# Third layer of a four-layer recurrent model: the passage into its loop over channel tiles is rebuilt, work for the second sequence and the routing move into single steps of the loop, and three operations of a step change their order or their size

## The reference

```python
proj = x @ W_in.T + b_in                    # gate 2048 | h 2048, B 128, C 128 | dt 32
conv = sum(xp[:, i:i + S, :] * conv_w[:, i] for i in range(4))   # h, B and C
h, Bm, Cm = split(silu(conv))
dt = softplus(dt + dt_bias);  Adt = -exp(A_log) * dt
A_cum = cumsum(Adt)                         # within a chunk
Y_diag = einsum((C @ B.T) * exp(segsum(Adt)), h * dt)
states = recurrence over chunks of einsum(B * exp(A_cum[-1] - A_cum), h * dt)
Y_off = einsum(C, states) * exp(A_cum)
g = (Y_diag + Y_off + D * h) * silu(gate)
g = g * rsqrt(mean(g * g) + EPS) * norm_w;  out = g @ W_out.T + b_out
# ffn: scores = sigmoid(x @ gate_W) * route_scale; the two largest, divided by their sum, weigh the experts
```

## Time and profile before

| | |
|---|---|
| median of 3 runs | 1264.71 us (1264.55 to 1265.39) |
| the profiled execution | 1266.14 us |
| its span | 1264.4 us |
| TensorE busy | 1134.3 us, 90% |
| VectorE busy | 899.1 us, 71% |
| ScalarE busy | 794.3 us, 63% |
| GpSimd busy | 564.4 us, 45% |
| mean granted clock | 0.96 of full speed |

### The profile page before, as it was taken

One profiled execution on the slowest core, in us unless ns is written; L12 is line 12 of the kernel. 1 busy time (PEld: TensorE's weight loads), 2 busy tenths in 40 slices (PEclk: granted clock), 3 DMA queues, 4 the chain that ended last, 5 costly groups with the idle time before them and its releaser, 6 DMA issues.

```text
span 1264.4 us, 14530 instructions
## 1 busy us (share of the span) xinstructions
PE 1134.3 (90%) x4940; PEld 611.8 (48%) x4940; DVE 899.1 (71%) x1361; ACT 794.3 (63%) x1118; POOL 564.4 (45%) x308
## 2 busy tenths in 40 slices
PE   6788999999989999999768999999999999897887
PEld 1333344444334444444446666666666666222554
DVE  3666999999974545434589989899899998323454
ACT  4467667667542433323578888888988887435542
POOL 6002899898933846431004545545455455200000
PEclk8879999999999999999789999999999999798999
DMA  3000655555442211110021212112111111000000
GB/s 124 1 1 19 221 183 176 196 177 188 171 160 59 60 42 42 36 45 1 1 72 30 59 52 59 52 44 59 52 55 55 44 59 37 1 0 1 1 1 34
DMA packets 36807, 84.22 MB, mean 67 GB/s; under 512 B 7253, under 2 KB 13174, under 8 KB 36470
## 3 DMA queue, kind: packets, MB, share of 16 engines
q1 hardware_dynamic: 36734, 83.29, 20.9%
HBM read 80.72 MB, written 2.56 MB: 66 GB/s over the span
## 4 chain that ended last, share of the span: by engine, by line
PE 43%; DVE 29%; ACT 15%; issue 7%; POOL 5%; DMA 1%; DVEq 0%; SPq 0%; POOLq 0%; ACTq 0%
DVE work L1572 7%; DVE work L660 6%; PE ps L1010 4%; PE ps L1267 4%; PE ps L1234 4%; PE ps L1026 3%; PE ps L1018 3%; DVE yd L1633 3%; ACT work L1430 3%; ACT work L1425 3%; ACT ps L557 3%; POOL work L721 2%; DVE work L1636 2%; PE ps L441 2%; PE ps L1841 2%
## 5 line engine op out<-in xcount | busy, mean ns | idle before, releaser
L1706 POOL TENSOR_TENSOR ssum<-ssum,rs 128x1024 f32<-128x1024 f32 x32 | 75.8, 2369 | 192.9 <-DVE work L1572 190.6
L660 DVE TENSOR_TENSOR_SCAN work<-ps,work 128x1024 f32<-128x1024 f32 x64 | 146.6, 2291 | 8.3
L1572 DVE SCALAR_TENSOR_TENSOR work<-work,w_t 128x1024 f32<-128x1024 f32 x96 | 123.3, 1285 | 33.6 <-ACT work L1430 31.3
L441 PE MATMUL ps<-work,ident 128*128 128x512 f32 x256 | 121.7, 598 | 5.6 <-POOL work L721 5.4
L1000 POOL TENSOR_TENSOR work<-work,ssum 128x1024 f32<-128x1024 f32 x32 | 76.3, 2389 | 108.9 <-DVE work L1089 56.4
L557 ACT ACTIVATE ps<-work,A 128x1024 f32<-128x1024 f32 x64 | 71.6, 1118 | 72.4 <-DVE work L660 72.4
L1089 DVE TENSOR_TENSOR work<-work,ps 128x512 f32<-128x512 f32 x64 | 43.8, 687 | 99.9 <-PE ps L1018 99.8
L1068 ACT ACTIVATE work<-ps 128x512 f32<-128x512 f32 x64 | 38.1, 597 | 115.4 <-PE ps L1010 115.3
L721 POOL TENSOR_TENSOR work<-work 128x1024 f32<-128x1024 f32 x42 | 99.1, 2362 | 13.5 <-DVE work L660 13.5
L1714 POOL TENSOR_TENSOR yd<-yd,work 128x896 f32<-128x896 f32 x32 | 67.0, 2094 | 70.2 <-DVE work L1636 70.2
L1623 DVE SCALAR_TENSOR_TENSOR work<-ps,work 128x512 f32<-128x512 f32 x128 | 81.9, 682 | 0.0
(11 more groups left out here) (349 smaller groups left out, 2546.6 us busy)
## 6 DMA issues: line engine op xcount, KB each, us to landing
work<-bc_rows SPq DMA_DIRECT2D x42, 512.0 KB, 3.5
work<-sdo_rows SPq DMA_DIRECT2D x64, 224.0 KB, 3.6
yd<-bc_rows SPq DMA_DIRECT2D x22, 512.0 KB, 3.7
rs<-w_rows SPq DMA_DIRECT2D x32, 256.0 KB, 4.1
ssum<-share_rows SPq DMA_DIRECT2D x32, 256.0 KB, 3.2
w_t<-in_tile_w SPq DMA_DIRECT2D x32, 195.5 KB, 2.5
work<-in_w SPq DMA_DIRECT2D x1, 2048.0 KB, 7.9
shared<-in_f SPq DMA_DIRECT2D x3, 512.0 KB, 5.9
```

The lines of the kernel that those rows point to most:

```text
L441: mm = pe.matmul(ps[:, YACC + h, :], ident[:, :], HS[u % 4][:, h * BL:(h + 1) * BL], start=(n == 0), stop=(n == DS - 1))
L660: dve.tensor_tensor_scan(h, flat_pair(DABANK), h, 0.0, ALU.mult, ALU.add).then_inc(m0["scan"], 1)
L1572: c = dve.scalar_tensor_tensor(HC[u], HP[:, tap:tap + SEQ], par(u, "taps", tap), HC[u], ALU.mult, ALU.add)
```

## The change

It has these parts.

1. *Products in the norm.* Step sizes and logits become one product of 40 columns (`w_dt` is now 32 plus 8 wide). The first two blocks of the B, C projection are computed while the norm runs.
2. *Routing.* The sigmoid becomes `1 / (1 + exp(-x))`; its exponential stays in the passage, and everything else of the routing moves into steps 17 to 24 of the loop (`beside`).
3. *Decays.* A matrix `later` gives the sum of the decays behind a position in one product, so that the copy and subtraction L1557, L1559 fall away; GpSimd builds it earlier on, in two short operations.
4. *First sequence only.* In the passage the turned sums, the three-part splits, decay rows, silu, transposes and products are done for the first sequence's eight chunks. The turned sums of the second sequence are computed in the passage too, behind the first's transposes; their splits come in steps 0 and 1 and their decay rows at the start of ScalarE's step 1.
5. *Second sequence in the loop.* First taps at the end of steps 2 and 3 (ScalarE), the six other taps in steps 3 to 8 (VectorE), silus in step 9 (ScalarE, between the silu of h and the exponentials), transposes in step 10 and products in step 11 (TensorE, ahead of the state products; the next projection of h waits there for ScalarE's copies or VectorE's mask).
6. *Order of a step.* VectorE's product with the decays stands ahead of the convolution. The silu of h is done in two halves. Both sets of four transposes stand together, each waiting for its half. GpSimd's sum waits for `yd` as well.

The diff, cut to its core:

```diff
-                for i in range(4 * k, 4 * k + 4):
-                    mm = pe.matmul(ps[:, DT_BANK, i * H2:(i + 1) * H2], tile(XN, i), W["w_dt"], start=True, stop=True)
+                    mm = pe.matmul(low[:, i // 8, i % 8, :], tile(XN, i), W["w_dt"], start=True, stop=True)
...
+            def while_normed(k):
+                if k == 0:
+                    project_bc(0, BACK)
+                if k == 1:
+                    steps_and_logits(0)
+                    steps_and_logits(1)
+                if k == 2:
+                    pe.wait_ge(m2["bc_pad"], 2)
+                    project_bc(1, BACK)
+                if k >= 2:
+                    steps_and_logits(k)
...
+            pe.matmul(ps[:, MID, :], later[:, :], adt, start=True, stop=True).then_inc(m2["pe"], 1)
+            pe.matmul(ps[:, MID + 1, :], ones_1[:, :], adt, start=True, stop=True).then_inc(m2["pe"], 1)
+            project_bc(2, LOW)
+            pe.wait_ge(m2["act"], m2["lndt"] + 1)
+            sums_turned(0)
+            pe.wait_ge(m2["bc_pad"], 6)
+            project_bc(3, LOW)
+            project_gate(0, 0, 0)
+            pe.wait_ge(m2["act"], m2["bc"] + 2)
+            # eight transposes of B, then
+            sums_turned(1)
+            # eight products of B and C, then
+            turn_h(0, 0, 0)
+            turn_h(0, 0, 1)
...
+                if n in (B1_TURN, B1_PRODUCT):
+                    second_sequence(n)
+                    from_states(n, b, 0)
+                    from_states(n, b, 1)
+                    if n == B1_TURN:
+                        pe.wait_ge(m2["act"], m2["bt_out1"] + 2)
+                    else:
+                        pe.wait_ge(m2["dve"], m2["gt_out1"] + 2)
                     project_h(m, b1, u1)
+                    within_chunks(n)
                     project_gate(m, b1, u1)
...
                 if more:
                     turn_h(m, u1, 0)
+                    turn_h(m, u1, 1)
                     pe.wait_ge(m2["yd"], n + 1)
                     arguments(m, u1, (0, 1))
-                    turn_h(m, u1, 1)
...
+            def silu_h(n, u):
                 act.wait_ge(m2["conv"], n + 1)
-                act.activation(HC[u], HC[u], ACT.Silu).then_inc(m2["hc"], 1)
+                for k in range(2):
+                    act.activation(blk(HC[u], k), blk(HC[u], k), ACT.Silu).then_inc(m2["hc"], 1)
...
             def step(n, b, t, u):
                 more = n + 1 < CT * BATCH
+                if n == 1:
+                    decay_rows(2)
+                    decay_rows(3)
+                if n == B1_TURN:
+                    b_turned(1)
...
+                    if n == B1_TURN - 1:
+                        bc_silu(1, 0)
+                        bc_silu(1, 1)
                     exponentials(n + 1)
                     weights_out(n + 1, 1 - u)
+                if n in (B1_CONV - 1, B1_CONV):
+                    bc_first_tap(1, n - B1_CONV + 1)
...
+            def beside(n):
+                if n < 2:
+                    three_parts(2 + n, ...)
+                elif B1_CONV <= n < B1_CONV + 2 * K3:
+                    m, i = divmod(n - B1_CONV, K3)
+                    dve.wait_ge(m2["bc_tap"], 3 + m)
+                    bc_tap(dve, 1, m, i)
+                elif n == B1_PRODUCT:
+                    mask_products(1)
+                elif n == ROUTE:
+                    # add 1, reciprocal, route_scale
+                elif n < ROUTE + 5 and n > ROUTE:
+                    top2_part(dve, own, rw[:, 0], rt[:, :, 0:E], *divmod(n - ROUTE - 1, 2))
+                # ROUTE + 5, + 6, + 7: share, weights, split in three
...
             def step(n, b, t, u):
                 m = n + 1
+                beside(n)
+                dve.wait_ge((m2["sdo_in0"], m2["sdo_in1"])[u], 32 * (n // 2 + 1))
+                dve.wait_ge(m2["yoff"], 2 * n + 2)
+                dve.tensor_tensor(Y[u][:, P:], Y[u][:, P:], flat2(MID)[:, P:], ALU.mult).then_inc(m2["ystar"], 1)
                 if m < CT * BATCH:
                     convolve(m, 1 - u)
...
-                dve.wait_ge((m2["sdo_in0"], m2["sdo_in1"])[u], 32 * (n // 2 + 1))
-                dve.wait_ge(m2["yoff"], 2 * n + 2)
-                dve.tensor_tensor(Y[u][:, P:], Y[u][:, P:], flat2(MID)[:, P:], ALU.mult).then_inc(m2["ystar"], 1)
...
                 pool.wait_ge(m2["ystar"], n + 1)
+                pool.wait_ge(m2["yd"], n + 1)
```

More of the change, by code:

```diff
@@ L290, in norm_act @@
             for k in range(NB):
+                if between is not None and k == NB - 1:
+                    between(0)
                 act.wait_ge(norm["centred"], NB * r + k + 1)
@@ L314, in top2 @@
                     own(dve.tensor_tensor(ind, ind, pick, ALU.add))
+        def top2(dve, own, score, ind):
+            for part in range(4):
+                top2_part(dve, own, score, ind, *divmod(part, 2))
         def split3(dve, own, w):
@@ L1294, in sum_out, with second_sequence @@
                 mm.then_inc(m2["outp"], 1)
+            def second_sequence(n):
+                pe.wait_ge(m2["act"], m2["bc1"] + 2)
+                for c in range(TB):
+                    if n == B1_TURN:
+                        mm = pe.transpose(four(FRONT + c // 4)[:, c % 4, :], tile(BCH[0], TB + c), ident[:, :])
+                    else:
+                        mm = pe.matmul(four(FRONT + c // 4)[:, c % 4, :], tile(BCH[0], TB + c), tile(BCH[1], TB + c), start=True, stop=True)
+                    if c % 4 == 3:
+                        mm.then_inc(m2["pe"], 1)
             def step(n, b, t, u):
@@ new lines, in while_normed, with sums_turned @@
+            def while_normed(k):
[9 more added lines that the diff above has]
+                    steps_and_logits(k)
+            def sums_turned(k):
+                for i in range(8 * k, 8 * k + 8):
+                    here = slice((i % 4) * P, (i % 4 + 1) * P)
+                    pe.matmul(ps[0:H2, 4 + i // 4, here], ADT[:, i, :], upper[:, :], start=True, stop=True)
+                    pe.matmul(ps[H2:2 * H2, 4 + i // 4, here], LNDT[:, i, :], ident[:, :], start=True, stop=False)
+                    mm = pe.matmul(ps[H2:2 * H2, 4 + i // 4, here], ADT[:, i, :], fall[:, :], start=False, stop=True)
+                mm.then_inc(m2["pe"], 1)
@@ L1365, in l2_pe @@
                 mm.then_inc(m2["pe"], 1)
[L1366 to L1376 removed]
+            pe.wait_ge(m2["bc_pad"], 8)
@@ L1377, in l2_pe @@
+            sums_turned(1)
+            pe.wait_ge(m2["act"], m2["cdec"] + 1)
+            for c in range(TB):
+                mm = pe.matmul(four(MID + c // 4)[:, c % 4, :], tile(BCH[0], c), tile(BCH[1], c), start=True, stop=True)
+                if c % 4 == 3:
+                    mm.then_inc(m2["pe"], 1)
+            turn_h(0, 0, 0)
+            turn_h(0, 0, 1)
+            pe.wait_ge(m2["act"], m2["bt_out"] + 2)
             arguments(0, 0, (0, 1))
```

281 lines of the change are left out of this document (145 added, 136 removed).

## The result

The kernel after took 1267.05 us in the median of 20 runs (1260.89 to 1269.35), the kernel before 1264.47 (1260.04 to 1266.37) beside it: ratio 1.0022, interval 1.0012 to 1.0033. So the change gains nothing; what it loses is between nothing and 0.3%. The forecast was 1263.3, 1.2 us faster. The profiled execution took 1266.82 us, with a span of 1264.9 and a mean granted clock of 0.968.

The account below looks back on a forecast made before the run. Bound by the chain across engines in the third layer's loop (13.20 us a step) and the passage ahead, not TensorE's 90% busy time. Minus 24.7 (passage) plus 23.3 (loop, tail) gave 1264.7 profiled, 1263.3 median; range 1257 to 1269.

Parts of the forecast that it names:

- The passage: From the norm's end to the first state product of the loop: 24.7 us shorter, that product at 631.6 us.
- six points: Steps of the passage sum, from step sizes and logits (603.0 us) to the first sequence's products and mask (631.6).
- point 3: Passage: two sums taken at 2.7 us, then B, C projection 1.8 and turned sums 3.55, reaching 615.9 us.
- The steady step: Plain step of the 32-tile loop: stays at 13.20 us to within 0.05; 0.02 taken off, 0.6 over the loop.
- Work beside steps: Second sequence's work and routing moved into single loop steps: lengthens them by 24.7 us together.
- Behind the loop: Program's end: GpSimd's last wait starts 1.0 us earlier; first state product 0.75 nearer the convolution's end.
- Clock at half behind 622 us in the passage: Rival: TensorE at half clock for transposes and turned chunks; 1267.8 us with 4.5 added; chance 0.2.
- A steady step that falls: Rival: in the loop up to 0.4 of 0.75 us comes through in some 20 steps, 1255 us; chance 0.15.
- The loop's order doing nothing: Rival: loop order has no effect and the passage runs at full clock: minus 3.8, 1260.9 us; chance 0.2.
- Late decays: Rival: decays land beyond 2.8 us of slack in lengthened steps, or step 11's mask waits longer; 1273; chance 0.07.
- The table load: ScalarE between silu and exponentials in a step: 1.28 us by the rows, not the skill's 2.66 for a switch.
- The sum of the forecast: Whole profile: minus 24.7 in the passage plus 23.3 in loop and tail, minus 1.4 against the profiled execution.

Follow-up runs that it names:

- experiments 3: Kernel before with only the three edits of the loop's order (product ahead of convolution, silu halves, joint transposes): 1265.22 us, ratio 0.9999 to the kernel before.
- experiment 4: Kernel after with the second sequence's decay rows in step 1 moved behind ScalarE's passes on the projection: 1263.83 us, ratio 0.9987 to the kernel before.
- experiment 7: Kernel after with silu whole and transposes apart again, product with the decays still ahead of the convolution: 1269.06 us, ratio 1.0046 to the kernel before.
- experiment 1: Kernel after with the product with the decays back behind the skip product, halves and joint transposes kept: 1251.36 us, ratio 0.9891 to the kernel before.
- the second: Comparison with both kernels run again unchanged: kernel after 1264.60 us against 1264.33, ratio 1.0007.

## Why the prediction was wrong

**The passage** was right: from the norm's end 24.8 and 25.1 us shorter, 24.7 forecast. Two of its six points were off and cancelled, which is luck: the logits ran at full clock, so that the decays were ready at 606.8 and not at 607.8, and the two sums of point 3 took 3.4 us and not 2.7 (windows of 0.84 and 0.73). TensorE had idled 3.12 us ahead of them, where 1.4 was reckoned with.

**The steady step** failed, and it is nearly all that the loop was missed by: "So the step stays at 13.20 us to within 0.05." The sum had 13.18. It is 13.36, in every kernel with the product in front of the convolution (experiments 3, 4, 7 and after), and 13.20 in each with it behind. In 31 steps the 0.18 make 5.6 us, of the 5.8 by which the loop of 438.9 stands above the 433.1 of the forecast. Count from C, the end of a convolution, 877.28 in the kernel after. TensorE, weight loads (PEld) of that step:

```profile
881.73 0.11 PEld L1252 LDWEIGHTS ps<-sel,spent 128*128 128x128 bf16 x2 [0.47 <-DVE work L1721]
882.06 0.30 PEld L1235 LDWEIGHTS ps<-work,w_t 128*128 128x128 f32 x2 [0.22 <-ACT work L1493]
```

and its matmuls:

```profile
882.06 1.98 PE L1235 MATMUL ps<-work,w_t 128*128 128x512 f32 x4
883.88 1.72 PE L1275 MATMUL ps<-work 128*128 128x128 f32 x14
```

The projection is released at C+4.78, as forecast (C+4.77). But I took the 3.46 us from there to the end of the state outputs out of the earlier trace rows, where they are counted from the first matmul, and before, the weights had been loaded 0.08 ahead of it. Weight loads of the kernel before:

```profile
804.34 0.30 PEld L1234 LDWEIGHTS ps<-work,w_t 128*128 128x128 f32 x2
```

From the weights on it is 3.54 in both. Then the product starts 0.10 behind the last matmul, which I had put at nothing (872.35 behind 872.25, one step earlier, where nothing stands beside the step). 4.78 plus 3.54, 0.10, 1.01 and 3.92 is 13.35. The forecast's own sum has a slip of 0.02 besides, the other way: 4.77 plus 3.46 is 8.23, not 8.25.

The prediction knows one way to the projection, over ScalarE's copies. There is a second, as long: in the chain shown above TensorE comes to the projection (L1235) from the exponentials (L1505), the masks (L1721) and the exponent arguments (L1252), and loads its weights at C+4.79 (868.70, C being 863.91). The Trainium skill (TensorE: Matmul & The Clock Gate, Step-by-step: what each phase is for) says that weight loads are pulled ahead of the matmuls in flight; the rows agree: the load at 804.34 comes while the matmuls of L1251 still run, from 803.99 to 804.59, and ahead of its own at 804.42. They show what it means for a sum: counted from a release, a group costs the load as well.

The halves and joint transposes bought nothing in a plain step. Without them, TensorE loads the projection's weights at C+4.78 too (883.46, C being 878.68 in experiment 7):

```profile
883.33 0.11 PEld L1252 LDWEIGHTS ps<-sel,spent 128*128 128x128 bf16 x2 [0.24 <-DVE work L1720]
883.46 0.30 PEld L1235 LDWEIGHTS ps<-work,w_t 128*128 128x128 f32 x2
```

What had held the projection at C+5.01 before was the product behind the skip product: with it there again and halves and joint transposes kept, it is at C+5.01 (experiment 1: 858.10, C being 853.09). What of the edits helps in steps with work beside them (0.2 us each) wasn't taken apart.

**Work beside steps.** Forecast 24.7 us in all, under the new order, less 0.5 in the first step; the loop has 24.7 over 31 plain steps of 13.36, so the sum was right. The six taps cost 4.9 (6.0 forecast), the steps with the second sequence's transposes and products took 17.99 and 17.61, 4.6 and 4.2 over a plain one (4.7, with the silus, and 4.3 forecast), the routing cost 4.8 (5.5). These were near. Interval 2 was 18.46, 5.1 over a plain one, where 2.7 was forecast: ScalarE's wait came as forecast, TensorE's slow passes behind its own wait had no place in the sum, and experiment 4 takes both away. In what stays there, 15.85, is the split, which the forecast has, and a low clock, which it lacks: in step 0 TensorE idles for 3.49 us, and its state shares (L1268, before L1267) then take 3.19 us, 3.17 in experiment 4, and not 1.80. What the prediction never asked is what the same work costs in the old order: the six taps 1.5, the routing 1.5 (experiment 1). Its own have the 1.00 us of idle time in front of the convolution that makes the difference; it noted only that 0.28 us is free in the new order, and it weighed the order edit as 0.02 us a step and nothing else. That is the error that matters for what the change is worth: the edit costs 13.0 us of the loop (5.0 in plain steps, 3.5 with the taps, 3.3 with the routing, 1.2 in the others together), 11 from the norm's end.

**Behind the loop** 1.0 was to be gained, or 0.25 counted from the last product; it was 4.4. Timeline of GpSimd behind the last step, kernel after, to be laid beside the earlier trace rows:

```profile
1080.93 2.07 POOL L1816 TENSOR_TENSOR yd<-yd,work 128x896 f32<-128x896 f32 x1 [1.22 <-DVE yd L1735]
```

Its wait fell from 2.33 to 1.22, as forecast; from the last L1591 to the last y it is 14.7 instead of 15.2. The other 3.9 goes with a lower clock of TensorE. Windows of TensorE from the last L1591 on, kernel before:

```profile
1081.80:1089.80 8.00, 6.97 (x12) 0.84 0.00 0
1089.80:1097.80 8.00, 6.81 (x8) 0.59 0.00 0
1097.80:1105.80 8.00, 8.00 (x15) 0.77 0.00 0
```

and the same places of the kernel after:

```profile
1086.68:1094.68 8.00, 5.01 (x10) 1.00 0.00 0
1094.68:1102.68 8.00, 7.24 (x16) 1.00 0.01 2
1102.68:1110.68 8.00, 8.00 (x18) 1.00 0.00 0
```

The stretch came the same in both profiles of each of the two kernels, and with the product in front it is 194.0 to 195.6 in all five profiles, with it behind 195.5 to 198.6 in eight. So the order may have a part in it; but the two groups meet, and in experiment 4 later decay rows in step 1 are all that differs from the kernel after, and it is 195.6 there, not 194.2. The waits ahead of the last L1292 are much alike, 2.65 us before and 2.35 after, and its four matmuls take 3.65 and 1.98. Why the clock falls in the one and not in the other stays open: no run changed the idle times there by themselves.

**The rivals.** Clock at half behind 622 us in the passage: it was 1.00. A steady step that falls: it rose. The loop's order doing nothing: it cost. Late decays: L1729 waited 13 times in the whole profile, 4.5 us together, each time for TensorE. The table load behaved as in the forecast: 1.28 us, with the exponentials 0.01 behind it; the longer switch of the Trainium skill (ScalarE: Activation LUTs, What ACT_TABLE_LOAD costs) isn't seen here either.

**The total.** The sum of the forecast was minus 1.4 on the profile. From the norm's end on the profiles have 665.1 and 665.2 before, 665.3 and 665.1 after, so it was missed by 1.4 us there. That it was no more is luck: the loop's 5.8 us beyond its 23.6 (24.7 less 0.6 and 0.5) and the 4.2 more given back at the end, for which the prediction had no term, nearly cancel. The medians stand 2.6 apart in the first comparison and 0.3 in the second. Some 0.3 lies outside the span (2.0 us in the mean of the runs after, 1.7 before); where the rest of the 2.6 lies, no profile shows.

## What to carry to other kernels

Before an operation is moved into an engine's wait, ask what else is to use that wait: here the same 1.00 us of VectorE was wanted by the moved product, which gained nothing there, and by the work taken out of the passage, and the product took it. Price an edit with the others already in: alone, on the kernel before, the order edit and its two companions read as no change (0.9999), though the loop was 5.0 us longer; on top of the new passage, taking the order back made 1251 us of 1265 to 1267. And cut profiles at rows that both kernels have, since the time ahead of the change varied here by more than the change itself was worth.

## What was not expected of the hardware

- Two profiles of the kernel before reached the norm's last block at 593.14 and 599.34 us, and were alike from there on to 0.1 us. The spans of one kernel tend to be shorter where its mean granted clock is higher: the kernel of experiment 1 ran at spans of 1253.0 (0.969) to 1245.9 (0.975).
- One wait of 2.12 us on TensorE was followed by four passes at 2.91 instead of 1.88 and 32 matmuls at 2.68 instead of 1.97, with the granted clock at 0.79 in 656 to 664. Without the wait (experiment 4) both took the shorter times.
- A group of matmuls that is released by a wait shows its matmul row at the start of its weight load (882.06 in both), one whose weights were loaded ahead shows it 0.08 to 0.10 later. Two rows of the same work, 1.98 and 1.90, cost the same from the release on.
